# Score rows of three attention heads by DMA instead of TensorE, value blocks one place forward, and the third layer's exponentials ahead of the copy of x, in a three-layer graph-attention kernel

## The reference

```python
mask = (adj > 0) | eye(512)
# layer 1: 4 heads of 128 features, x is 512 x 256
xl   = (x @ W1)                                   # 512 x 4 x 128
e    = leaky(asrc[s, h] + adst[d, h], 0.2); e = where(mask[s, d], e, -1e9)
h    = elu(softmax(e, axis=s)^T @ xl + b1)        # 512 x 512
# layer 2: the same with one head of 256 features (W2), no elu
x    = layernorm(x + layer2(h))
# layer 3: one head of 256, mask is adj > 0, softmax over the other axis of the same matrix
x    = layernorm(x + leaky(layer3(x)))
```

## Time and profile before

| what | value |
|---|---|
| median of 3 runs | 991.84 us (990.63 to 991.93) |
| profiled execution, device time | 991.7 us |
| its span, first to last instruction | 989.9 us |
| busy: PE, DVE, ACT, POOL | 877.5, 740.5, 685.3, 272.4 us |
| mean granted TensorE clock | 0.97 |
| from one graph to the next, steady part | 55.3 us |

### The profile page before, as it was taken

The page is one execution under the profiler, slowest core; times in us unless marked ns, Lnnn a source line. Parts: engine busy times, 40 slices in busy tenths (PEclk is TensorE's granted clock), DMA queues, the critical chain, the costliest instruction groups (busy, mean ns, idle before and its releaser), DMA issues.

```text
span 989.9 us, 17244 instructions
## 1 busy us (share of the span) xinstructions
PE 877.5 (89%) x6216; PEld 821.0 (83%) x6216; DVE 740.5 (75%) x1875; ACT 685.3 (69%) x1267; POOL 272.4 (28%) x255
## 2 busy tenths in 40 slices
PE   0687989999999999999999999999999999998654
PEld 0576979898998989898998989898999989897543
DVE  4666677878787888878787888879787888875430
ACT  1375758778686877778686877778686878875530
POOL 0001001024231422424232412424233313324353
PEclk9997989999999999999999999999999999999886
DMA  6323020201203040301203040301102010000000
GB/s 187 82 67 86 1 85 2 59 28 33 76 22 86 1 107 2 102 7 40 68 22 86 1 107 2 107 2 46 63 22 86 2 43 1 22 1 22 23 22 21
DMA packets 63000, 45.56 MB, mean 46 GB/s; under 512 B 35778, under 2 KB 54338, under 8 KB 62916
## 3 DMA queue, kind: packets, MB, share of 16 engines
q1 hardware_dynamic: 62916, 44.45, 15.8%
HBM read 27.66 MB, written 8.39 MB: 36 GB/s over the span
## 4 chain that ended last, share of the span: by engine, by line
PE 51%; DVE 21%; ACT 16%; issue 6%; POOL 5%; DMA 1%; SPq 0%; POOLq 0%; DVEq 0%; ACTq 0%
PE bU L471 11%; PE bU L450 9%; PE bG L533 8%; PE bU L461 7%; PE bG L519 6%; ACT att L596 6%; DVE junk L734 5%; ACT att L607 4%; POOL val3s L365 3%; ACT x L619 3%; PE bB L410 3%; DVE low L747 2%; PE bA L410 2%; DVE stats L812 2%; PE bG L530 2%
## 5 line engine op out<-in xcount | busy, mean ns | idle before, releaser
L734 DVE CUSTOM_DVE_ANT_0 junk<-mask_t,bA,val 128x512 bf16<-128x512 bf16 x320 | 219.8, 743 | 44.0 <-PE bA L410 40.5
L450 PE MATMUL bU<-val,att 128*128 128x129 f32 x2048 | 249.6, 275 | 3.3 <-DVE att L778 3.3
L450 PEld LDWEIGHTS bU<-val,att 128*128 128x128 f32 x2048 | 241.4, 192 | 5.7 <-issue 3.4
L778 DVE SCALAR_TENSOR_TENSOR att<-mask_n,att 128x2048 f32<-128x2048 bf16 x80 | 183.4, 2292 | 81.5 <-ACT att L607 81.3
L596 ACT ACTIVATE att<-bB,val 128x512 f32<-128x512 f32 x320 | 202.6, 708 | 1.3 <-PE bB L410 1.3
L607 ACT ACTIVATE att<-att 128x2048 f32<-128x2048 f32 x80 | 155.3, 1941 | 0.7
L471 PE MATMUL bU<-val3s,att 128*128 128x256 f32 x512 | 119.2, 387 | 23.7 <-POOL val3s L365 23.7
L471 PEld LDWEIGHTS bU<-val3s,att 128*128 128x128 f32 x512 | 97.0, 194 | 39.3 <-DVE res L806 16.0
L461 PE MATMUL bU<-val,att 128*128 128x257 f32 x512 | 120.1, 388 | 9.4 <-DVE att L778 9.4
L461 PEld LDWEIGHTS bU<-val,att 128*128 128x128 f32 x512 | 97.1, 195 | 23.4 <-DVE att L778 9.9
L659 ACT COPY val<-bG 128x524 f32<-128x524 f32 x64 | 38.7, 605 | 111.6 <-PE bG L533 111.6
(11 more groups left out here) (82 smaller groups left out, 1592.1 us busy)
## 6 DMA issues: line engine op xcount, KB each, us to landing
adj_in<-in_adj_dram SPq DMA_DIRECT2D x16, 1024.0 KB, 5.8
x_in<-in_x_dram SPq DMA_DIRECT2D x16, 512.0 KB, 6.7
out_dram<-act SPq DMA_DIRECT2D x16, 512.0 KB, 2.9
mask_t<-mask_n SPq DMA_TRANSPOSE x64, 2.5
att<-in_L_gnn_W_dram SPq DMA_DIRECT2D x4, 128.0 KB, 2.4
att<-in_L_gnn_W_dram SPq DMA_DIRECT2D x1, 512.0 KB, 8.1
att<-in_L_gnn_att_src_dram SPq DMA_DIRECT2D x1, 256.0 KB, 5.3
att<-in_L_gnn_att_dst_dram SPq DMA_DIRECT2D x1, 256.0 KB, 7.6
```

The costliest lines, as they stand in the source:

```text
L450: ins = nc.tensor.matmul(to[:, (d % 2) * FX:(d % 2 + 1) * FX], p[:, s, d * P:(d + 1) * P], val1[u.batch % 2][:, s, u.index // 2, values], ...
L734: nc.vector.tensor_tensor_reduce(junk[:, b] if u.row else att[u.slot % 3][:, b], mask_t[u.batch % 4][:, b], bA[:], 1.0, a_col(u, b) if u.r ...
L778: nc.vector.scalar_tensor_tensor(flat(p), mask_n[u.batch % 3][:, 0:NB * N], BIG, flat(p), ALU.add, ALU.min)\
```

## The change

The heads h1, h2 and h3 (`by_dma`) no longer have their row of scores spread by PE into `bA`. SP writes their columns to a DRAM tensor (`store_scores`: three DMAs for blocks 0 to 2, three for block 3) and reads them back with one DMA that gives all 128 partitions the three rows, 6 KB each, in a new SBUF tile `a_rows` (`spread_rows`). `tops` of these heads reads `a_rows` where it read `bA`. Blocks 0 to 3 of `values_1` now come in slots 1 (ahead of the attention of the third layer), 1, 2 and 5. In slot 0 ACT makes the third layer's exponentials before it copies x, and DVE does `invert_3` before `make_mask` and `x_low`.

```diff
         self.row = kind != "L3"
+        self.by_dma = kind == "h" and index > 0
 def gat_kernel(nc, x, adj, W1, as1, ad1, b1, W2, as2, ad2, b2, W3, a3, out):
...
         u.r = i
+    for i, u in enumerate(u for u in units.values() if not u.by_dma):
+        u.a = i
...
+        a_rows = sb("a_rows", [P, H - 1, N])
+        a_dram = nc.dram_tensor("a_rows_dram", (H - 1, N), F32).ap()
         low = sb("low", [P, NB])
...
         bias2_ready = sem("bias2_ready")
         adj_loaded = sem("adj_loaded")
+        a_stored = sem("a_stored")
+        a_spread = sem("a_spread")
...
                 if n >= 4:
                     sp.wait_ge(res1_done, (n - 3) * NB)
                 sp.dma_start(x_in[n % 4][:], x[n].rearrange("(b p) f -> p b f", p=P)).then_inc(x_loaded[n % 4], 16)
+            def store_scores(n, blocks):
+                sp.wait_ge(val1_ready, n * NB + blocks.stop)
+                if n:
+                    sp.wait_ge(a_spread, 16 * n)
+                for h in range(1, H):
+                    with nc.allow_non_contiguous_dma(reason="columns of scores"):
+                        sp.dma_start(a_dram[h - 1].rearrange("(b p) -> p b", p=P)[:, blocks],
+                                     val1[n % 2][:, blocks, h // 2, HC + h % 2]).then_inc(a_stored, 16)
+            def spread_rows(n):
+                sp.wait_ge(a_stored, (n + 1) * 2 * (H - 1) * 16)
+                if n:
+                    sp.wait_ge(top_done, (units[SLOTS * (n - 1) + H].u + 1) * NB)
+                sp.dma_start(a_rows[:].rearrange("p h n -> p (h n)"),
+                             a_dram.rearrange("(o h) n -> o (h n)", o=1).to_broadcast([P, (H - 1) * N]))\
+                    .then_inc(a_spread, 16)
...
                     load_adj(n + 2)
                 if 2 <= n + 2 < B:
                     load_x(n + 2)
+                if 0 <= n + 1 < B:
+                    store_scores(n + 1, slice(0, 3))
                 if 0 <= n - 3 < B:
                     sp.wait_ge(y_out_done, (n - 2) * NB)
                     sp.dma_start(out[n - 3].rearrange("(b p) f -> p b f", p=P), y_out[:]).then_inc(out_stored, 16)
+                if 0 <= n + 1 < B:
+                    store_scores(n + 1, slice(3, 4))
+                    spread_rows(n + 1)
             sp.wait_ge(out_stored, 16 * B)
...
                     pe.wait_ge(val2_ready, (u.batch + 1) * NB)
                 else:
                     pe.wait_ge(val3_ready, (u.batch + 1) * NB)
-                if u.u:
-                    pe.wait_ge(top_done, u.u * NB)
+                before = [v for v in units.values() if not v.by_dma and v.a == u.a - 1]
+                if before:
+                    pe.wait_ge(top_done, (before[0].u + 1) * NB)
                 spread(bA, lambda b: a_col(u, b), arow_done)
             def targets_row(u):
...
                     weight_sums()
                 if pos == 0 and batch:
                     turn_x(n + 1)
+                if pos == 1 and batch:
+                    if n == -1:
+                        pe.wait_ge(w1_lo_ready, 1)
+                        pe.wait_ge(bias1_ready, 2 * G)
+                    values_1(n + 1, 0)
                 if pos == 2 and batch:
-                    values_1(n + 1, 1)
+                    values_1(n + 1, 2)
                 if pos == 3 and second:
                     values_2(n - 1, (2, 3))
                 if pos == 4 and third:
                     values_3(n - 2, (0, 1))
                 if pos == 5 and batch:
-                    values_1(n + 1, 2)
+                    values_1(n + 1, 3)
                 if before:
                     attend(before, 0)
                 if oldest:
...
                 if after and after.row:
                     targets_row(after)
                 if pos == 1 and batch:
-                    if n == -1:
-                        pe.wait_ge(w1_lo_ready, 1)
-                        pe.wait_ge(bias1_ready, 2 * G)
-                    values_1(n + 1, 0)
+                    values_1(n + 1, 1)
                 if pos == 2 and second:
                     if n == 1:
                         pe.wait_ge(w2_lo_ready, 1)
...
                     turn_x1(n - 2)
                 if pos == 4 and third:
                     values_3(n - 2, (2, 3))
-                if pos == 5 and batch:
-                    values_1(n + 1, 3)
                 if before:
                     attend(before, 1)
-                if later:
+                if later and not later.by_dma:
                     sources_row(later)
...
                     normalize(older)
                 if this:
                     leaky(this, (2, 3))
-                if pos == 0 and batch:
-                    x_out(n + 1)
+                if pos == 1 and batch:
+                    values_1_out(n + 1, 0)
                 if pos == 2 and batch:
-                    values_1_out(n + 1, 1)
+                    values_1_out(n + 1, 2)
                 if pos == 3 and second:
                     values_2_out(n - 1, (2, 3))
                 if pos == 4 and third:
                     values_3_out(n - 2, (0, 1))
                 if pos == 5 and batch:
-                    values_1_out(n + 1, 2)
+                    values_1_out(n + 1, 3)
                 if this:
                     exps(this)
-                if pos == 5 and batch:
-                    values_1_out(n + 1, 3)
+                if pos == 0 and batch:
+                    x_out(n + 1)
                 if pos == 1 and batch:
-                    values_1_out(n + 1, 0)
+                    values_1_out(n + 1, 1)
                 if third_layer:
                     third_out(third_layer, 1)
                 if pos == 2 and second:
...
             def tops(u):
-                dve.wait_ge(arow_done, u.u + 1)
+                if u.by_dma:
+                    dve.wait_ge(a_spread, 16 * (u.batch + 1))
+                else:
+                    dve.wait_ge(arow_done, u.a + 1)
+                a_row = a_rows[:, u.index - 1] if u.by_dma else bA[:]
                 if u.kind == "h" and u.index == 0:
                     dve.wait_ge(mt_loaded, (u.batch + 1) * NB * 16)
                 for b in range(NB):
                     nc.vector.tensor_tensor_reduce(junk[:, b] if u.row else att[u.slot % 3][:, b], mask_t[u.batch % 4][:, b],
-                                                   bA[:], 1.0, a_col(u, b) if u.row else LOWEST, ALU.add, ALU.max,
+                                                   a_row, 1.0, a_col(u, b) if u.row else LOWEST, ALU.add, ALU.max,
                                                    top[u.u % 2][:, b:b + 1]).then_inc(top_done, 1)
             def shifted_targets(u):
...
                     second_out(units[g - 1], 0)
                 if g == 0:
                     shift_bias_2()
+                if this and not this.row:
+                    invert_3(this.batch)
                 if pos == 0 and 0 <= n + 1 < B:
                     make_mask(n + 1)
                     x_low(n + 1)
                 if this and this.row:
                     keep_edges(this)
-                elif this:
-                    invert_3(this.batch)
                 if oldest and pos != 1:
                     low_part(oldest)
                 if older:
```

## The result

| | before | after |
|---|---|---|
| median | 991.24 us (988.6 to 991.93) | 1143.4 us (1142.89 to 1144.22) |
| span of the profiled execution | 989.9 us | 1141.1 us |
| mean granted TensorE clock | 0.970 | 0.916 |
| from one graph to the next, mean of the last eight | 55.2 us | 66.5 us |

The ratio is 1.1539 (95%: 1.1516 to 1.1563). The direction is as forecast. The size, +152 us, lies far outside the range, whose end was 1,075 us. The last row of the table is the spacing of SP's issues of the loads of x.

A forecast was written before the change was run, and what follows sets the result against it. PE nearly full (53.26 of 55.30 us), but DVE and POOL set part of the period: 20.76 + 21.5 + 0.4 + 14.9 = 57.6, with the clock 59.1; +3.8 in 12 graphs, +3 at edges: 1,040 us, range 1,000 to 1,075.

The forecast's parts named there:

- The step that failed: SP's three stores of the last block's scores: landing assumed 2.9 us after issue, like the store of out.
- both bounds to the spread: Spread of score rows to all partitions: 4.4 us or 8.3 us, stalling PE by 0 or 3.8 us; 0.4 taken.
- E to V: From end of masking the second layer's matrix to PE's attention of h0 in slot 2: 21.5 us plus 0.4 stall.
- blocked and the spread late too: Rival: POOL blocks tops of h3 and the spread lands late, two gaps a graph; about 1,090 us, chance 0.08.
- My line for what would prove me wrong: Sign against the forecast: DVE's longest wait is tops of h1 waiting for the spread.
- V to B: From PE's attention of h0 in slot 2 to end of h3's b_t: POOL's additions exclude tops, 14.9 us against 12.24.
- B to E: From end of h3's b_t to the next masking of the second layer's matrix: same chain, unchanged at 20.76 us.
- the 45.6 of my sum: Whole per-graph change, +3.8 us, over the 12 graphs where POOL's three additions meet tops of h3: +45.6 us.
- The clock: TensorE clock falls to 0.50 at the 3.3 us gap before h3's targets, in three of four graphs: 1.5 us a graph.
- My 0.8 us from E to V: New order with three fewer PE row spreads a graph: E to V shortens by 0.8 us to 21.5.
- If PE set everything, the period would fall to about 52: Removing three row spreads (1.32 us) and filling PE waits of 1.1 and 0.7 us would cut 55.30 to about 52.
- The ramp: Edges, +3 us: graph 2 +2, graph 15 +1.5, first spread unhidden +2, first three graphs' saved transposes -2.5.

The follow-up runs named there:

- e12_spaced: Changed kernel, but from graph 1 on the last block's scores are stored 64 bytes apart into a tensor nobody reads; 1041.69 us.
- e1_spread_first: Changed kernel, but SP stores the last block and spreads the rows before it waits for norm_2 and stores out; 1046.9 us.
- e8_apart: e1_spread_first with POOL's three additions taken apart: one at the start of slot 0, one in slot 2, one in slot 3; 999.1 us.
- e7_fill: Changed kernel, with the four transposes of h3's output made nine times over in slot 1, before PE's wait for h1's targets; 1129.42 us.
- e4_order_only: Changed kernel with its new order on ACT, DVE and PE, but no row by DMA, all rows by PE; 988.42 us.
- e13_dma_from_3: e8_apart with the rows of the first three graphs by PE; SP stores and spreads only from graph 3 on; 981.09 us.
- e9_apart_pairs: e8_apart with scores stored as 8-byte pairs, 16 bytes apart in each of two DMAs, read by DVE with a step of four elements; 1016.11 us.
- e2_h3_by_pe: Changed kernel, but the row of h3 comes by PE through bA again; h1 and h2 stay with DMA; 1075.6 us.
- m1_stores: No computation, one kind of store at a time, each awaited: 128 4-byte elements took 7.2 us touching, 1.4 us at 64 or more bytes apart.
- m2_spacing: As m1_stores, with other distances: 4-byte elements 8, 16 and 32 bytes apart took 2.8, 2.3 and 1.4 us in the first round.
- e10_pairs: Changed kernel with scores stored as 8-byte pairs, 16 bytes apart in each of two DMAs, read by DVE with a step of four elements; 1120.34 us.

## Why the prediction was wrong, step by step

**The step that failed** is the one that read: "The trace has no store of single 4-byte elements. I give them a landing as late as that of the store of `out`, 2.9". The landing is 8.3 us behind the last issue in the kernel (7.2 to 10.0 over the steady graphs), and 7.2 from issue to landing for one column alone. The operation had no row, and I put one value on it, from a row that shares nothing with it but the direction. I gave both bounds to the spread, which then landed about as assumed: 4.8 us after its issue (5.5 on the median), where I had 4.4 plus a reserve. From this one term followed:

- *E to V*, forecast 21.9, measured 29.9 (486.94 - 457.00). `bB` of h1 comes 5.2 us later than in my chain, which is its gap. Behind it the 7.3 us of work took 10.1, with PE at 0.50 for the first 5: 2.8 us. Together 8.0. Shown by `e12_spaced`: with only the last block's stores spaced apart, 102 us of 152 go.
- The rival "blocked and the spread late too" had this picture, two gaps and 1,090 us, at 0.08. It was still 53 us short, because its lateness came from the bandwidth of the spread, at most 3.8 us, and it had one clock term for two gaps. That bound does not come out of its own terms either: 5.4 + 8.3 is 13.7, not 15, which makes a stall of 2.6. My line for what would prove me wrong, a wait of `tops` of h1 for the spread as the longest of DVE, is what the waits show (5.8 us).

**V to B** was right: forecast 14.9, measured 14.70 (501.64 - 486.94). `tops` of `a_rows` and the additions exclude each other: 2.10, 1.64 and 2.83 us beside POOL, 0.74 alone. In this the trace agrees with the Trainium skill, "SBUF — State Buffer", section "Who interferes with whom", by which the second of two such instructions to start is held until the first has ended. In price: 48 us between `e1_spread_first` and `e8_apart`. The 45.6 of my sum stood for the whole per-graph change, so the agreement in size is in part chance.

**B to E** was right: 20.76, measured 522.40 - 501.64 = 20.76. What PE no longer does in slots 4 and 5 was not won while `b_t` of h3 was late.

**The clock** was right in kind and wrong in place. I had it fall in front of h3 in three of four graphs. In the twelve graphs of after with that gap (3.0 to 3.3 us) it fell fully in three and in part in two. The fall in front of h1, which I did not have, came in all twelve. `e7_fill` gives a lower bound for both: 14 us, with 512 added transposes, most of which lie in a gap.

**The order** by itself did nothing for the period (55.25 against 55.18 in `e4_order_only`). My 0.8 us from E to V counted on the transposes of h1 to h3 being gone as well. "If PE set everything, the period would fall to about 52" was not reached by any kernel. The best period was 54.3.

**The ramp** was under-estimated. I had +3 us at the edges. `e8_apart` and `e13_dma_from_3` differ by 18 us, though the first has the shorter period (54.3 against 54.7). That it is the DMA rows of the first three graphs is shown. With stores that land sooner the fifth load of x comes 11 us earlier, at 149.2 in `e12_spaced` against 160.5 in after and at 149.8 in `e9_apart_pairs` against 161.2 in `e8_apart`, where the kernel before has 141.8. So more than half of it is the same landing. The rest was not followed up.

**The range** had bounds for the spread, the block and the clock, and none for the landing of the stores. The chain as written down would have shown how much hangs on it: 2.7 to the last issue, 8.3 of landing and 4.4 of spread make E + 15.4, against the 11.1 by which `tops` of h1 must start, a stall of 4.3 us. The stores were also issued 0.8 us later than I had them (460.51, E + 3.5), and the spread took 0.4 more: E + 16.6.

**Still open**: the last 17 of the 68 us of `e2_h3_by_pe`, what the clock costs apart from the gaps that it comes with, and whether rows by DMA win anything over rows by PE once order and POOL are as in `e13_dma_from_3`. Why touching writes land late was not looked into: the runs show the times only. Spaced scores were never read back (`e12_spaced` does not), so no run shows a layout that is quick to store and quick for DVE to read.

## What to carry to other kernels

What the small stores cost here was set by how their pieces lie in DRAM, not by their bytes: 0.5 KB in touching elements landed in 7.2 us, 64 KB in rows of 512 bytes in 1.5. A DMA on the critical path that the trace has never shown wants a measurement or a wide bound. Store and spread as soon as the data is there, and do not queue them behind an unrelated wait on the same issuing engine: that was 96 us here. Before the input of a DVE instruction moves from PSUM to SBUF, look at what POOL does at that time, and spread POOL's two-input work out: that alone won 0.5% in the kernel before.

## What the runs showed of the hardware

- A store of 128 touching 4-byte elements to DRAM takes 7.2 to 7.5 us to its landing (`m1_stores`), three of 384 elements 9.9 to 10.1 behind the last issue, with a DMA share of 0.00 to 0.02 meanwhile. At 8 bytes apart it is 2.8, at 16 bytes 2.3 and 1.4, at 32 bytes and more 1.4 (`m2_spacing`, `m1_stores`). Touching pieces of 8 bytes take 3.3 to 3.5, of 16 bytes 1.4 to 1.7.
- A DVE instruction of two inputs over 512 columns (the masked maximum of `tops`) takes 0.74 us whether its second input is in PSUM or in SBUF, but 1.10 to 1.27 when that input is float32 with a step of four elements (`e10_pairs`, `e9_apart_pairs`).
- DVE and POOL, each with a row of instructions with two SBUF inputs, alternate instruction by instruction, and both are stretched: from 0.74 to between 1.64 and 2.83 us on DVE, from 1.17 to 1.62 and from 2.36 to 2.80 on POOL.
- A gap of 3.00 us before the same four transposes ends at 0.65 us in some graphs and at 1.11 in others: five full falls of twelve in `e1_spread_first`, three in after. In `e7_fill`, where PE does more ahead of it, the four transposes behind this gap never took over 0.86 us. In `e2_h3_by_pe` eleven gaps of 3.5 to 5.4 us ended at 1.11 and one of 3.88 at 0.65. The length of the gap alone does not decide.
